# Layer norm statistics of the first FFN on ScalarE, one power for both norms, and a shorter last sum on GpSimd

## The reference, cut to what matters

```python
x = x + attn_a(_layernorm(x))   # 16 heads of 8, log-sparse mask: 8 or 9 offsets a row
x = x + ffn(_layernorm(x))      # v = _layernorm(x): aff = v @ centroids.T, expert = argmax(aff)
                                # y = v + relu(LN(v) @ w1.T + b1) @ w2.T + b2
                                # alpha = sigmoid(aff of the expert); alpha * y + (1 - alpha) * v
x = x + attn_b(_layernorm(x))   # 16 heads of 64, causal
x = x + ffn(_layernorm(x))      # the same ffn
def _layernorm(x, eps=1e-5): m, v = mean(x), var(x); return (x - m) / sqrt(v + eps)
```

## Time and profile before

| | |
|---|---|
| time, median of 3 runs | 528.8 us (528.21 to 530.34) |
| the profiled execution | 524.73 us, span of its core 522.9 us |
| busy: PE, PE weight load, DVE, ACT, POOL | 433.8, 340.7, 370.5, 253.6, 239.0 us |
| mean granted clock of TensorE | 0.918 of 2.4 GHz |

### The profile page before, as it was taken

The page is one execution under the profiler, slowest core; times in us unless marked ns, Lnnn a source line. Parts: engine busy times, 40 slices in busy tenths (PEclk is TensorE's granted clock), DMA queues, the critical chain, the costliest instruction groups (busy, mean ns, idle before and its releaser), DMA issues.

```text
span 522.9 us, 11650 instructions
## 1 busy us (share of the span) xinstructions
PE 433.8 (83%) x3882; PEld 340.7 (65%) x3882; DVE 370.5 (71%) x1466; ACT 253.6 (49%) x867; POOL 239.0 (46%) x250
## 2 busy tenths in 40 slices
PE   2857896634999289999999999999999998439993
PEld 1324555523999246787777778777776787339992
DVE  6699998961666358857779687796879776456661
ACT  1641000512444037758757678576774857115450
POOL 6100988471455224544435345463445546314453
PEclk9987999555999689999999999999999999859997
DMA  8999930034673200000000000000000000136640
GB/s 310 359 389 422 419 158 1 22 106 118 213 207 116 85 2 2 1 1 3 1 1 4 1 1 13 11 21 3 1 11 12 22 1 22 42 101 203 195 140 6
DMA packets 22234, 48.98 MB, mean 94 GB/s; under 512 B 3328, under 2 KB 13574, under 8 KB 19744
## 3 DMA queue, kind: packets, MB, share of 16 engines
q1 hardware_dynamic: 18880, 40.86, 22.3%
q0 software_dynamic: 3296, 7.39, 4.5%
HBM read 24.99 MB, written 24.15 MB: 94 GB/s over the span
## 4 chain that ended last, share of the span: by engine, by line
PE 62%; DVE 17%; issue 6%; ACT 5%; POOL 5%; DMA 3%; POOLq 0%; SPq 0%; DVEq 0%; ACTq 0%
PE ps L868 9%; PE ps L881 8%; PE ps L924 8%; PE ps L999 6%; PE ps L1012 6%; PE ps L966 5%; PE ps L941 4%; PE ps L931 4%; ACT vT L657 3%; PE ps L758 3%; POOL vT L520 2%; PE ps L776 2%; PE ps L716 2%; POOL sorted_in L490 2%; DVE prod L1110 2%
## 5 line engine op out<-in xcount | busy, mean ns | idle before, releaser
L520 POOL TENSOR_TENSOR vT<-vT,prec 128x256 f32<-128x256 f32 (+1 forms) x128 | 103.1, 826 | 129.5 <-DVE prec L1446 128.7
L657 ACT ACTIVATE vT<-vT,nmax 128x128 f32<-128x128 f32 (+1 forms) x256 | 113.4, 448 | 14.3 <-DVE nmax L1436 14.1
L1436 DVE CUSTOM_DVE_ANT_0 vT<-ps,cst 128x128 f32<-128x128 f32 (+1 forms) x256 | 77.5, 350 | 5.4 <-PE ps L966 5.3
L665 ACT COPY prod<-ps 128x384 f32<-128x384 f32 x96 | 42.9, 482 | 60.6 <-PE ps L999 60.6
L924 PE MATMUL ps<-xnT,wb 128*128 128x256 f32 x256 | 68.0, 389 | 1.4 <-DVE qk L1417 0.9
L999 PEld LDWEIGHTS ps<-cst,vT 128*128 128x128 f32 x384 | 42.7, 141 | 30.7 <-POOL vT L520 15.3
L999 PE MATMUL ps<-cst,vT 128*128 128x128 f32 x384 | 54.5, 278 | 4.1 <-POOL vT L520 3.1
L1417 DVE COPY qk<-ps 128x512 f32<-128x512 f32 x64 | 43.4, 678 | 13.6 <-PE ps L924 13.5
L881 PE MATMUL ps<-w2s,pv 128*128 (+1 forms) x368 | 49.3, 277 | 0.8 <-issue 0.8
L924 PEld LDWEIGHTS ps<-xnT,wb 128*128 128x128 f32 x256 | 44.8, 195 | 7.6 <-DVE qk L1417 2.4
L657 ACT ACTIVATION_READ_ACCUMULATOR vT<-vT,nmax 128x1 f32 x256 | 49.0, 191 | 0.0
(11 more groups left out here) (150 smaller groups left out, 794.6 us busy)
## 6 DMA issues: line engine op xcount, KB each, us to landing
sorted_in<-zero SPq DMA_DIRECT2D x1, 16512.0 KB, 64.8
pv<-in_w SPq DMA_DIRECT2D x30, 259.0 KB, 4.0
pv<-sorted_in SPq DMA_DIRECT2D x46, 129.0 KB, 2.8
wps<-in_w SPq DMA_DIRECT2D x1, 2072.0 KB, 9.4
w2s<-in_w SPq DMA_DIRECT2D x1, 2048.0 KB, 14.1
wb<-in_w_b SPq DMA_DIRECT2D x1, 1536.0 KB, 22.9
xres<-in_x SPq DMA_DIRECT2D x4, 256.0 KB, 3.9
xres<-in_bo_a POOLq DMA_DIRECT2D x2, 512.0 KB, 13.8
```

The lines of the kernel that those rows point to most:

```text
L520: last = nc.gpsimd.tensor_tensor(px, px, view(prec, m_at(n, x) + t * 2, [[1, 2], [0, (t + 1) * P]]), ALU.mult)
L657: last = nc.scalar.activation(px, px, ACT.Exp, bias=nmax[:, m:m + 1], scale=-1.0, accum_out=psum[:, m:m + 1])
L1436: ins = nc.vector.tensor_tensor_reduce(out=pb[:, o:o + w], in0=wide[:, c:c + w], in1=cst[:, mask:mask + w], scale=-1.0, scalar=-MASKED * 2 ...
```

## The change

- On ACT, a new `moments(g)` for the groups 0, 1 and 2 of the first FFN stands behind attention a's `exps_a` and ahead of the first `residual`. It waits for `a_x` of g + 1, forms the sums of four tiles by four Identity activations with accumulator, mean and negative mean by two Copy activations of 4 columns, the squares about the mean by four Square activations with accumulator, and the two halves of `vv` by two Identity activations of 4 columns; it raises the new semaphore `f_va`. The token numbers go into `pack` on ACT too.
- `vv` now holds var + eps and var·(1+eps) + eps². The inverse root of the latter is the factor of both norms at once, since it is (var+eps)·(var/(var+eps) + eps). So `spread` on DVE, for the last group of the first FFN and all groups of the second, is two instructions without a wait between them instead of four with waits; `norm` has as many instructions as before.
- In the last round of attention a (r = 7) POOL stops at `sum4`, and PE projects four sums instead of two for each batch.
- DVE's order: `norm(0)`, `residual_a(3)`, `means`/`spread(3)`, `choose`/`count(0)`, `norm(1)`, `place(0)`, `norm(2)`, and from there as before.

```diff
@@ gpsimd, add_up(r)
-                own.after(nc.gpsimd.tensor_tensor(view(sum4, 0, [[4 * P, 2], [1, 4 * P]]),
+                ins = nc.gpsimd.tensor_tensor(view(sum4, 0, [[4 * P, 2], [1, 4 * P]]),
...
+                if r == NR - 1:
+                    ins.then_inc(a_sum, 1)
+                    return
+                own.after(ins)
@@ powers(k, g)
-                pool.wait_ge(f_ve, k * NG + g + 1)
+                if k == 0 and g < NG - 1:
+                    pool.wait_ge(f_va, g + 1)
+                else:
+                    pool.wait_ge(f_ve, 1 if k == 0 else g + 2)
@@ scalar, behind exps_a
+            def moments(g):
+                lo, n = GROUPS[0][g]
+                own = slice(lo, lo + n)
+                act.wait_ge(a_x, g + 1)
+                for t in range(lo, lo + n):
+                    last = nc.scalar.activation(xn[:, (t - lo) * D:(t - lo + 1) * D], xres[:, t * D:(t + 1) * D],
+                                                ACT.Identity, accum_out=sum1[:, t:t + 1])
+                fa.after(last)
+                nc.scalar.activation(view(fmv, 2 * lo, [[2, n]]), sum1[:, own], ACT.Copy, scale=1.0 / D)
+                fa.after(nc.scalar.activation(less_mean[:, own], sum1[:, own], ACT.Copy, scale=-1.0 / D))
+                for t in range(lo, lo + n):
+                    last = nc.scalar.activation(xn[:, UL + (t - lo) * D:UL + (t - lo + 1) * D],
+                                                xres[:, t * D:(t + 1) * D], ACT.Square,
+                                                bias=less_mean[:, t:t + 1], accum_out=sumsq[:, t:t + 1])
+                fa.after(last)
+                nc.scalar.activation(vv[:, 2 * lo:2 * lo + n], sumsq[:, own], ACT.Identity, bias=epss[:, 0:1],
+                                     scale=1.0 / D)
+                nc.scalar.activation(vv[:, 2 * lo + n:2 * lo + 2 * n], sumsq[:, own], ACT.Identity, bias=epss[:, 1:2],
+                                     scale=(1.0 + EPS) / D).then_inc(f_va, 1)
+
+            nc.scalar.copy(view(pack, 2 * D + 1, [[ROW, NT]]), cst[:, C_TOKEN:C_TOKEN + NT])
+            for g in range(NG - 1):
+                moments(g)
@@ tensor, out_a(r)
+                    if r == NR - 1:
+                        slots = [sum4[:, (4 * j + s) * P:(4 * j + s + 1) * P] for s in range(4)]
@@ vector, spread(k, g) and norm(k, g)
-                fo.after(nc.vector.tensor_scalar(one, var, EPS, None, ALU.add))
-                fo.after(nc.vector.reciprocal(rv[:, lo:lo + n], one))
-                fo.after(nc.vector.tensor_tensor(var2[:, lo:lo + n], var, rv[:, lo:lo + n], ALU.mult))
-                nc.vector.tensor_scalar(two, var2[:, lo:lo + n], EPS, None, ALU.add).then_inc(f_ve, 1)
+                nc.vector.tensor_scalar(one, var, EPS, None, ALU.add)
+                nc.vector.tensor_scalar(two, var, 1.0 + EPS, EPS * EPS, ALU.mult, ALU.add).then_inc(f_ve, 1)
...
-                nc.vector.tensor_tensor(both[:, own], r1, r2, ALU.mult)
+                nc.vector.tensor_tensor(both[:, own], vv[:, 2 * lo + n:2 * lo + 2 * n], r2, ALU.mult)
...
-                nc.vector.tensor_tensor(root2[:, own], vv[:, 2 * lo + n:2 * lo + 2 * n], r2,
-                                        ALU.mult).then_inc(f_cf, 1)
+                nc.vector.tensor_tensor(root2[:, own], both[:, own], r1, ALU.mult).then_inc(f_cf, 1)
@@ vector, the order ahead of the first FFN
-            nc.vector.tensor_copy(view(pack, 2 * D + 1, [[ROW, NT]]), cst[:, C_TOKEN:C_TOKEN + NT])
-            dve.wait_ge(a_x, NU - 1)
-            for g in range(2):
-                means(0, g)
-                spread(0, g)
+            norm(0, 0)
             residual_a(NU - 1)
-            norm(0, 0)
-            means(0, 2)
-            spread(0, 2)
-            norm(0, 1)
-            choose(0, 0)
-            count(0, 0)
             dve.wait_ge(a_x, NU)
             means(0, 3)
             spread(0, 3)
+            choose(0, 0)
+            count(0, 0)
+            norm(0, 1)
             place(0, 0)
```

More of the change, by code:

```diff
@@ L218, in hybrid_layer @@
         rr = sb("rr", [P, 2 * NT])
-        rv = sb("rv", [P, NT])
-        var2 = sb("var2", [P, NT])
+        sum1 = sb("sum1", [P, NT])
+        sumsq = sb("sumsq", [P, NT])
+        less_mean = sb("less_mean", [P, NT])
+        epss = sb("epss", [P, 2])
         both = sb("both", [P, NT])
@@ L280, in hybrid_layer @@
         (f_ve, f_rs, f_cf, f_vh, f_res, f_vT, f_vTs, f_aff, f_oh, f_am, f_ea, f_al, f_rank, f_row, f_hs, f_total,
-         f_tab, f_sent, f_tx, f_xs, f_h, f_ha, f_hv, f_y, f_ys) = sems(
-            "f_", "ve rs cf vh res vT vTs aff oh am ea al rank row hs total tab sent tx xs h ha hv y ys")
+         f_tab, f_sent, f_tx, f_xs, f_h, f_ha, f_hv, f_y, f_ys, f_va) = sems(
+            "f_", "ve rs cf vh res vT vTs aff oh am ea al rank row hs total tab sent tx xs h ha hv y ys va")
         f_ld, f_wl = [sem(f"f_ld{i}") for i in range(XR)], [sem(f"f_wl{i}") for i in range(WR)]
@@ L286, in hybrid_layer @@
          b_z, b_o, b_x) = sems("b_", "w xn xT xTs j qk vp v s mx e r n t pa pd pv z o x")
-        own_ln, own_sm, own_sum, own_f = sems("own_", "ln sm sum f")
+        own_ln, own_sm, own_sum, own_f, own_v = sems("own_", "ln sm sum f v")
         block = ctx.enter_context(nc.Block())
@@ L440, in _ @@
             nc.gpsimd.memset(mhalf[:], -0.5)
+            nc.gpsimd.memset(epss[:, 0:1], EPS)
+            nc.gpsimd.memset(epss[:, 1:2], EPS * EPS)
             nc.gpsimd.memset(view(kT, 0, [[W_A, NB], [1, P]]), 0.0)
@@ L463, in add_up @@
                 o = r % RP * 2 * SLOTS * P
-                own.after(nc.gpsimd.tensor_tensor(view(sum4, 0, [[4 * P, 2], [1, 4 * P]]),
-                                                  view(pv, o, [[SLOTS * P, 2], [1, 4 * P]]),
-                                                  view(pv, o + 4 * P, [[SLOTS * P, 2], [1, 4 * P]]), ALU.add))
+                ins = nc.gpsimd.tensor_tensor(view(sum4, 0, [[4 * P, 2], [1, 4 * P]]),
+                                              view(pv, o, [[SLOTS * P, 2], [1, 4 * P]]),
+                                              view(pv, o + 4 * P, [[SLOTS * P, 2], [1, 4 * P]]), ALU.add)
+                if r == NR - 1:
+                    ins.then_inc(a_sum, 1)
+                    return
+                own.after(ins)
                 need(pool, a_y, r - RP + 1)
@@ L590, in _ @@
                 exps_a(t)
+            fa = Own(act, own_v, 100)
+            fa.turn(0)
+            def moments(g):
[20 more added lines that the diff above has]
+                moments(g)
             def residual(k, g):
@@ L1243, in norm @@
                     last = nc.vector.tensor_scalar(pack[:, t * ROW:t * ROW + D], xres[:, x:x + D],
-                                                   fmv[:, 2 * t:2 * t + 1], both[:, t:t + 1], ALU.subtract, ALU.mult)
+                                                   fmv[:, 2 * t:2 * t + 1], rr[:, lo + n + t:lo + n + t + 1],
+                                                   ALU.subtract, ALU.mult)
                 last.then_inc(f_vh, 1)
```

## The result

The change made the kernel faster by 0.7%: 525.73 us median (524.16 to 526.63, 6 runs) against 528.76 (528.21 to 530.68, 6 runs), ratio 0.9932 with a 95% interval of 0.9908 to 0.9956. The forecast was 525.5, 3.3 us less than before; 3.0 us came.

A forecast was written before the change was run, and what follows sets the result against it. POOL's 16 back-to-back dispatches were taken to bound the first FFN's preparation. First dispatch 2.4, tail 0.5 and attention b 0.4 sum to 3.3 us: 528.8 to 525.5 us, range 523.9 to 528.6.

The forecast's parts named there:

- First dispatch: First FFN's preparation: POOL's first dispatch starts at 98.0 instead of 100.44 us, 2.4 us earlier (1.4 to 3.1 by clock).
- moments(2): Group 2's statistics on ACT, behind residual_a(2), take 4.1 us (ends 3.5 and 5.5); ACT is free at 88.3.
- Rivals 3 and 5: ACT table loads: 3, a second load ahead of exps(0), 526.6 us, chance 0.06; 5, reloads each function change, 531.7, 0.05.
- Powers 0 to 2: On POOL, one after another behind its last sum, 85.6 to 90.7 us, 1.67 each; norm(0) waits for power 0.
- rival 2: POOL's powers hold norm(0) until power 1 ends; residual_a(3) 1.2 us later, gain 2.1 us, 526.7; chance 0.06.
- Rival 1: PE's clock is low from the start of affinity(0), and attention b gives nothing: gain 1.9 us, 526.9; chance 0.22.
- Alpha of group 0: First FFN's preparation: complete with place(0) at 97.2 us; POOL's first dispatch then starts 0.8 us later.
- Groups 2 and 3 have over 3 us: First FFN: later groups keep ahead of POOL, so 16 dispatches stay back to back and the gain reaches L858 whole.
- Short sum: Attention a's end: without POOL's second level PE starts 1.35 us earlier but does more matmuls; gain 0.45 us.
- Tail: Second FFN's preparation: the last group's spread loses two instructions and two waits; 0.5 us, all on the path.
- Attention b: Shorter spread there: steps 10 and 18 give nothing, step 24 a little; 0.4 us (ends 0 and 1.3).
- Rival 4: First dispatch is set by something both kernels have; only the tail's 0.5 us is left, 528.3 us; chance 0.08.

The follow-up runs named there:

- e1: The kernel before, profiled and timed again with no edit; ratio to before 1.0011 (0.9983 to 1.004).
- e2: The changed kernel, profiled and timed again with no edit; ratio to before 0.9939 (0.9916 to 0.9962).
- e6: e3 with one more wait: POOL starts all dispatches only behind the last alpha; 530.46 us, ratio to before 1.0009.
- e3: The changed kernel with norm(1) put ahead of choose(0) and count(0) on DVE; 521.0 us, ratio to before 0.9874.
- e5: The changed kernel with the full second level of the sum back in round 7; ratio to before 0.9954.
- e4: The kernel before with the new factor alone (short spread, one power for both norms), statistics and order as before; 524.68 us, ratio 0.9936.
- e8: e6 with 12 extra indirect DMAs issued by POOL into spare DRAM while DVE prepares groups 1 to 3; 540.68 us (one run).
- e9: e6 with 12 extra plain DMAs from POOL's queue while DVE prepares groups 1 to 3; 530.85 us (one run).
- e10: e6 with 16 extra plain DMAs from SP's queue, two in flight, while DVE prepares groups 1 to 3; 531.55 us (one run).
- e11: e6 with eight extra powers of 128x8 on POOL, no DMA, while DVE prepares groups 1 to 3; 533.41 us (one run).

## Why the prediction came out right, point by point

**First dispatch, forecast 2.4 us earlier.** Right: 16.27 us behind `residual_a(2)` in before, 13.92 in after (2.35 less); against e1 it is 2.8 to 3.2. The steps on the way:

- *moments(2)* took 3.80 us, 85.89 to 89.69, where 4.1 were forecast. ACT's timeline, after, answers to the earlier trace rows:

```profile
85.89 0.31 ACT L612 ACTIVATE xn<-xres 128x128 f32<-128x128 f32 x1 [4.61 <-DVE xres L1211]
86.10 0.19 ACT L612 ACTIVATION_READ_ACCUMULATOR xn<-xres 128x1 f32 x1
86.19 0.29 ACT L612 ACTIVATE xn<-xres 128x128 f32<-128x128 f32 x1
...
87.93 0.39 ACT L618 ACTIVATE xn<-xres,less_mean 128x128 f32<-128x128 f32 x1
...
89.41 0.28 ACT L624 ACTIVATE vv<-sumsq,epss 128x4 f32<-128x4 f32 x1
```

An Identity with its accumulator read goes at 0.30 us from start to start, a Square with a bias from memory at 0.39; the row that I took, 0.40, has that second form. ACT loaded one table, 1.28 us at 0.74 as in the earlier trace rows, and none here, so Square needs no other than exp. Rivals 3 and 5 are out. The Trainium skill, ScalarE: Activation LUTs, section "Table sets: the hidden batching unit", leaves that open; the trace settles it for this pair.
- *Powers 0 to 2* ran as one row of 4.88 us, 1.63 each, right behind the last sum, as forecast. `norm(0)` began 3.01 us behind `residual_a(2)`; forecast 3.11. Its `both` took 0.16 us with a power beside it. So rival 2 is out, and the rule of the Trainium skill, GPSIMD Engine Reference, section 1 (Specifications), on DVE instructions with two SBUF inputs does not hold beside a power here. It holds beside POOL's division in attention b, below.
- *PE's last round* took 2.94 us, 87.27 to 90.21; forecast 2.95.
- *The clock.* `affinity(0)` took 1.06 us (forecast 0.94) and began at 2.4 GHz, `turn_v(1)` 1.11 at 1.2 GHz. Windows, after, answering to the earlier trace rows: the granted clock fell within the 94th microsecond, one later than in before. Rival 1's first half is out.

```profile
92.00:93.00 1.00, 0.62 (x6) 0.62 (x6) 0.55 (x6) 0.32 (x1) 0.38 (x2) 1.00 0.00 0
93.00:94.00 1.00, 0.43 (x4) 0.34 (x4) 0.46 (x3) 0.00 (x0) 1.00 (x1) 0.73 0.00 0
```

- *Alpha of group 0* came at 98.84, 12.99 us behind `residual_a(2)`; forecast 13.03. POOL started 0.93 us later, forecast 0.8.

**"Groups 2 and 3 have over 3 us. So 16 dispatches stay back to back and the gain reaches L858 whole."** This step failed. The prediction had named its sign, POOL waiting for a later group's row, and POOL waited 3.79 us for the alpha of group 3. L858 was forecast at 122.4, 38.2 us behind `residual_a(2)`; PE started there at 41.59 and, in e2, 41.02. The chain that ended last, after, goes where the earlier trace rows has only dispatches:

```profile
105.74 2.73 another core or an unknown queue
...
109.40 4.04 another core or an unknown queue
...
115.07 1.96 another core or an unknown queue
...
118.04 0.73 issue
118.77 0.96 POOL sorted_in L501
...
127.44 0.49 PE ps L899
```

The last alpha decides, not the first dispatch, and three late hand-overs stand ahead of it. In the work itself the step was sound: e6, without them, has the last alpha 22.2 us behind `residual_a(2)`, in time for the 13th dispatch of e3's pace (11.07 + 12 x 1.27 = 26.3 us). With them e3 has it at 28.35. I read POOL as the bound from one execution that had no late hand-over. The 4.1 us between it and the median, which I left in as a constant, were in part these: e1's span is 5.2 us longer, 1.65 of it ahead of the end of `residual_a(2)` and 2.77 between there and L858.

The forecast was met all the same, because the late hand-overs hold before (e1, 8.16 us) nearly as much as after (8.81 and 8.65). The earlier start of the chain is passed on to the last alpha, less about that difference: e1's PE starts 43.43 us behind `residual_a(2)`, after's 41.59 and 41.02. That is 1.8 to 2.4 us, where 2.4 were forecast. The size is right by another way than the one forecast, and that is in part luck: between before and e1, the same program, the late hand-overs come with 2.77 us at PE's start, more than the whole term.

**Short sum, forecast 0.45.** Mis-sized, though the 2.4 us did not rest on it: they were worked out from the time of power 0. In the new order `norm(0)` waits for power 0, which stands behind POOL's last sum, so the whole 1.35 us of the second level counts there. I had placed power 0 by that sum, but had priced the sum by PE's end. e5 gives 1.35 us of wait and 1.7 to 2.0 at the first dispatch; in its time the ratios are 0.15% apart, unresolved.

**Tail, forecast 0.5.** Right: from the last `xres` to the last group's first dispatch 9.68 us in before, 9.16 in after, and 9.15 to 9.17 in e2 to e4. The chain, after, answering to the earlier trace rows:

```profile
452.22 0.17 DVE vv L1266
452.39 0.08 DVE vv L1267
...
459.38 0.74 issue
```

**Attention b, forecast 0.4.** Mis-sized: 1.03. From the first to the 61st reciprocal of DVE's softmax it took 238.96 us in before and 237.93 in after (238.98 in e1, 237.90 in e4, so it is the new factor's). Up to step 18 the two agree within 0.03 us; half comes behind step 18, half behind step 24. I had taken `norm` as unchanged, and missed that its `both` was held up there too. DVE's timeline of before in step 18, and PE's gap behind it, then DVE's of after; no such gap of PE stands there in after:

```profile
349.07 1.59 DVE L1235 TENSOR_TENSOR both<-rr 128x4 f32<-128x4 f32 x1
```
```profile
352.69 1.13 PE L931 MATMUL ps<-wb,xnT 128*128 128x512 f32 x2 [0.26 <-DVE prod L1422]
```
```profile
350.77 0.22 DVE L1274 TENSOR_TENSOR both<-vv,rr 128x4 f32<-128x4 f32 x1
...
350.99 1.00 DVE L1276 SCALAR_TENSOR_TENSOR shift<-fmv,rr 128x4 f32<-128x4 f32 x1
```

POOL's two divisions run beside both rows, from 349.02 to 350.64 in before and from 350.37 to 351.97 in after. The hold did not go: it moved from `both` to `shift` and became shorter, so that the four small instructions of `norm` took 1.42 us instead of 1.93. Behind step 24 `both` stayed held (1.36 and 1.22 us). Of PE's gaps three went, 0.26, 0.18 and 0.19 us; that is 0.63 of the 1.03 us, and the rest is not accounted for. The held `spread` of step 10 (0.74 us) gave nothing, as forecast: PE was busy.

**Sum.** By the traces 1.8 to 2.4, 0.5 and 1.0 us, 3.4 to 3.9 against e1's execution; the medians differ by 3.0 and 2.7. Each is from single executions, and the late hand-overs alone differ by up to 0.65 us between them. Rival 4 is out, since all three terms are there.

## What to carry to other kernels

Take a second profile of the kernel before when the profiled execution is not near its median: what it lacks may be the bound. In a stretch with a run of indirect DMAs on POOL, count the waits of DVE on PE that fall beside it, and bring forward what the last of them needs, not only what the first dispatch needs. When a chain waits twice for short times, as here 0.89 and 1.43 us, ask which ready work of the same engine could stand in the first wait: exchanging `norm(1)` with `choose(0)` was worth as much by the ratios (0.65% against 0.61%) as the rest of the change.

## What the runs showed of the hardware

- While POOL issued a run of indirect DMAs (1.27 us from start to start), the semaphores of PE that DVE waited for rose 0.5 to 7.5 us behind the modelled end of the product, at the first of DVE's waits later than 5.7 us after the first DMA and at those behind it. DVE lost 0.49 to 4.77 us at each, 8.81 in after, 8.16 in e1, 8.67 in e8 (two waits). The profiled execution of before had none with such DMAs; e6, e9, e10 and e11 had none without them beside the preparation, e9 with the limit told above. Hand-overs from DVE to PE and ACT in that stretch were prompt in after (0.06 and 0.03 us). The eight traces with late hand-overs also lack many records of semaphores there.
- The first indirect DMA starts 0.93 us (after) and 0.94 us (e3) behind the alpha that releases it.
- A power of 128x8 on POOL (1.63 us) did not hold up a DVE instruction with two SBUF inputs (0.16); POOL's division of 128x256 did (1.59 and 1.36 us in before, 1.22 and 1.00 in after).
